# Real and imaginary products summed in DRAM by accumulating transfers, in a fused attention and spectral filter kernel

## The chip, the cores and the metric

The kernel runs on one core of one Trainium2 chip. The metric is the device time of one execution in microseconds (us). Times of single instructions come from one profiled execution.

## The reference, cut to what matters

The kernel computes a neighbourhood attention block with an MLP over x of shape (4, 56, 56, 128), a gated attention over the same rows, and a spectral filter bank. The change touches only the last part:

```
Vf = rfft(phi, n=8192);  Uf_p = rfft(u, n=8192);  Uf_m = rfft(u * sgn, n=8192)
U_plus  = irfft(Vf * Uf_p)[:, :sl]
U_minus = irfft(Vf * Uf_m)[:, :sl] * sgn
out = einsum('btkd,k,kde->bte', U_plus, sigma ** 0.25, M_phi_plus)
    + einsum('btkd,k,kde->bte', U_minus, sigma ** 0.25, M_phi_minus)
    + (three shifted products with M_u)
```

One of four filter sets is chosen by a softmax over weights and noise. The kernel works in the frequency domain: for each frequency s it forms a complex 128x128 matrix G(s) from phi, sigma and the M matrices, multiplies the spectrum U(s) of the rows by it, and transforms the products Y(s) back. Y is complex. Its real part is rU rG - iU iG and its imaginary part rU iG + iU rG, so four real products go into two sums.

## The kernel before, in words

The order of the work is written out by hand, one list per stage, and every engine walks the same list. Four stages follow each other: the front (attention, MLP), the spectrum of the rows, the filter stage (class Filters, L1313 to L1526), from about 870 to 1634 us, and the inverse (class Inverse, L1560 to L1871), to the end.

**Filter stage.** 784 frequencies (slots) lie in 14 groups P of 56. A group has four steps s (56 steps in all): two halves of the output columns e, and two of the filter sets each. In a step PE makes 32 filter tiles G (L1379, L1382), ACT and DVE copy them from PSUM by turns (L1420, L1434), and PE multiplies U by them in 28 sums (L1401). The four products of a slot are not combined: the rows of a sum are U's real and imaginary part apart (p, r, b), its columns are G's real and imaginary part (k, e). After each odd step ACT copies the four PSUM banks of sums to the tile YS (L1426), and SP stores YS by four transfers of 224 KB to the DRAM tensor Yd (L1498), 28 stores in all. POOL prepares U with its twiddle factors (planes, L1451 to L1479) for 28 half groups. The tile for U has three buffers.

**Inverse.** Eight groups n (batch b, pair pp) of the rows have two steps t = 2n, 2n+1 each. For n the slots of Yd are loaded into YL[n % 2] by eight transfers of 392 KB (load_y, L1529). For n = 0 and 1 they are issued in the filter stage, the last rows of them after the last store has landed. For later n SP issues them when the buffer is free. DVE combines YL into YC (L1707): one addition or subtraction of 98x1024 for each of two halves and two parts k, and a copy of row 0 for its special slots (L1711). POOL forms sums and differences BF of the odd slots (butterfly, L1733), for n = 0 DVE does the second half. In step t PE does:

- turn(t-1) (L1628), a reversal of rows of the tile DF, after the odd part of t;
- the even part (L1608): banks "two" and "four", from YC;
- the odd part (L1621): banks "straight" and "crossed", from BF.

ACT copies "two" (PB, L1692) and scales the odd banks (SP, L1678, L1680), POOL adds these to DVE's GH (outer, L1761, L1762) in EO (L1839). DVE's loop over t runs in this order: whole(t-1), which makes SC (L1770), DF (L1775) and NT (L1776); outer(t); turned(t-2) (L1795); kept(t-1) (L1786); then a combine. kept and turned add the result to the tile RN, which holds the rows of the attention part; kept(2n) waits until RN(n) has been loaded (load_out, L1545, 2 x 392 KB). ACT stores RN(n-1) in step t = 2n+1 (L1850).

In SP's list of the inverse, step n waits for the combines of n, issues the loads of n+2, waits for the store of RN(n-2) and issues load_out(n).

Of the kernel before, what the change touches and what calls it, by code (L numbers as in the profile page):

```python
# [11 lines left out]
G = 98  # L12
# [225 lines left out]
class Front:  # L238
# [222 lines left out]
    def load_columns(self, e):  # L461
# [8 lines left out]
        e.dma_start(col[:, 6:10], D["b_fc1"].rearrange("(i p) -> p i", p=128), allow_slow_non_contiguous=True).then_inc(S["d_rest"], 16)  # L470
        for i, a in enumerate((D["b_proj"], D["b_fc2"], D["bq"], D["bk"], D["bv"])):
            e.dma_start(self.rowb[:, 1 + i, :], row_of(a)).then_inc(S["d_rest"], 16)

    def scalar(self, e):
        S, col = self.S, self.col
        for k, n in self.order:
# [83 lines left out]
            elif k == "p_pick":  # L560
                e.wait_ge(S["pz"], 1)
                e.activation(self.tm[:, 4:8], self.tm[:, 0:4], ACT.Exp, accum_out=self.tm[:, 17:18]).then_inc(S["pexp"], 1)
# [11 lines left out]
            elif k == "p_root":  # L574
                for i in range(2):
                    if i == 0:
                        e.wait_ge(S["d_pick"], 16 * 7)
                    else:
                        e.wait_ge(S["root"], 1)
                    e.activation(self.sg[:, i + 1:i + 2], self.sg[:, i:i + 1], ACT.Sqrt).then_inc(S["sqrt"], 1)  # L580
            elif k in ("f_dft", "f_part"):
                self.spec.scalar(e, k, n)
            elif k == "p_vf":
                e.wait_ge(S["vmul"], 2 * n + 2)
                if n == 0:
                    e.wait_ge(S["root"], 2)
# [27 lines left out]
    def vector(self, v):  # L614
        S, ch = self.S, self.dve_steps
        for k, n in self.order:
# [121 lines left out]
            elif k == "p_root":  # L738
                sg = self.sg
                for i in range(2):  # L740
                    s, r = sg[:, i:i + 1], sg[:, i + 1:i + 2]
                    v.wait_ge(S["sqrt"], i + 1)
# [8 lines left out]
                    v.tensor_scalar(r, r, 0.5, None, ALU.mult).then_inc(S["root"], 1)  # L751
# [17 lines left out]
    def pick(self, v):  # L769
# [8 lines left out]
        v.tensor_scalar(z, z, tm[:, 16:17], None, ALU.subtract).then_inc(S["pz"], 1)  # L778
        v.wait_ge(S["pexp"], 1)
# [151 lines left out]
    n_rest = 16 * (2 + 1 + 5 + 3 + 3)  # L931

    def setup(self, e, part):
# [15 lines left out]
        e.dma_start(self.ident[:, :], D["c_id"]).then_inc(S["d_first"], 16)  # L949
# [134 lines left out]
    pz pexp mixed mturn cast rest sqrt root vmul vf vcut  # L1084
# [228 lines left out]
class Filters:  # L1313
# [44 lines left out]
    def tensor(self, e):  # L1358
        S = self.S
        for k, s, i in self.order():  # L1360
# [24 lines left out]
            elif k == "sums":  # L1385
# [10 lines left out]
                if par == 0 and i % 8 == 0 and s >= 2:  # L1396
                    e.wait_ge(S["ys"], 4 * (s // 2 - 1) + bk + 1)
# [17 lines left out]
    def scalar(self, e):  # L1415
        S = self.S
        for k, s, i in self.order():
# [33 lines left out]
    def planes(self, q, c, u, u7, w, n):  # L1451

        S, ch = self.S, self.pool_steps
        a = u7.rearrange("d s (m r b) -> d s m r b", m=7, r=2)[:, :, 0:3]
# [24 lines left out]
        q.tensor_tensor(im, im, spare, ALU.subtract).then_inc(S["u7"], 1)  # L1479

# [533 lines left out]
```

## Time and profile before

| | |
|---|---|
| median of 3 runs | 1827.38 us (1826.96 to 1833.2) |
| profiled execution, its own time | 1826.17 us |
| its span | 1824.9 us |
| mean granted TensorE clock | 0.964 |
| PE, DVE, ACT, POOL busy | 1696.0, 1352.8, 1228.7, 727.5 us |

Engines: PE is TensorE's matmul, PEld its weight load, DVE is VectorE, ACT ScalarE, POOL GpSimd, SP SyncE. SPq and ACTq are DMA issues of these engines. A row's line number (L1401) is that of the kernel before. "idle before <-" names what ended the idle time before an instruction. "issue" there is time in which the engine waited for nothing that the profile shows. PEclk is the granted TensorE clock, where 1.00 is 2.4 GHz and 0.50 is 1.2 GHz. DMA share is the mean busy share of the 16 DMA engines.

### The profile page before, as it was taken

How to read it: one execution, taken by the hardware profiler on the slowest of the kernel's cores; microseconds unless marked ns; L12 is line 12 of the kernel's file. 1: busy time of each engine (PE TensorE's matmuls, PEld its weight loads, DVE VectorE, ACT ScalarE, POOL GpSimd, SP SyncE). 2: the span in 40 equal slices, each digit the busy share in tenths (PEclk: the TensorE clock that was granted, in tenths of full speed). 3: DMA queues.
4: the chain of work that ended last, by engine and by line, in shares of the span. 5: the costliest groups of instructions: out<-in, count | busy, mean ns of one | idle time of the engine just before them, and what ended most of it. 6: DMA issues, size and time to landing. Idle time of an engine off the chain costs nothing.

```text
span 1824.9 us, 76133 instructions
## 1 busy us (share of the span) xinstructions
PE 1696.0 (93%) x32219; PEld 1355.5 (74%) x32219; DVE 1352.8 (74%) x3789; ACT 1228.7 (67%) x2667; POOL 727.5 (40%) x877
## 2 busy tenths in 40 slices
PE   5999999999999998989899999999999999986887
PEld 3566676666766766888788888888888888874555
DVE  2677778888867765795677777777777777747998
ACT  5788888887877754646677777777777777751221
POOL 6545556555645543130532213333222333104553
PEclk8899999999999997998999999999999999997888
DMA  4422333433233323386322122222212222268763
GB/s 118 116 80 76 106 85 93 110 85 99 75 86 92 85 72 91 110 275 209 118 68 56 37 69 69 63 53 59 64 40 69 68 57 59 58 162 218 221 194 105
DMA packets 266056, 181.12 MB, mean 99 GB/s; under 512 B 39944, under 2 KB 263078, under 8 KB 264218
## 3 DMA queue, kind: packets, MB, share of 16 engines
q1 hardware_dynamic: 257154, 169.07, 33.8%
q10 hardware_dynamic: 7924, 6.02, 1.1%
q8 instruction: 256, 4.19, 1.0%
q0 software_dynamic: 640, 1.16, 0.2%
q14 instruction: 82, 0.67, 0.1%
HBM read 105.65 MB, written 70.63 MB: 97 GB/s over the span
## 4 chain that ended last, share of the span: by engine, by line
PE 63%; DVE 16%; issue 9%; POOL 5%; ACT 4%; DMA 2%; SPq 1%; DVEq 0%; POOLq 0%; ACTq 0%
PE banks L1401 19%; PE banks L1379 10%; PE banks L1382 9%; PE banks L409 6%; DVE zone L610 4%; PE banks L403 3%; PE banks L368 2%; PE banks L358 2%; PE banks L416 2%; PE banks L382 1%; DVE YC L1707 1%; PE banks L1608 1%; PE banks L456 1%; DVE st L597 1%; DVE W L652 1%
## 5 line engine op out<-in xcount | busy, mean ns | idle before, releaser
L1434 DVE COPY Gm<-banks 128x448 f32<-128x448 f32 x896 | 552.8, 639 | 206.9 <-PE banks L1379 126.7
L1420 ACT ACTIVATE Gm<-banks 128x448 f32<-128x448 f32 x896 | 515.2, 628 | 195.3 <-PE banks L1379 149.1
L1401 PE MATMUL banks<-Gm,U 128*32 128x128 f32 x12544 | 514.4, 274 | 9.7 <-POOL U L1479 5.1
L1401 PEld LDWEIGHTS banks<-Gm,U 128*32 128x32 f32 x12544 | 336.6, 110 | 53.0 <-issue 48.1
L1382 PE MATMUL banks<-V,zone 118*32 118x224 bf16 x7040 | 292.3, 259 | 0.0
L872 POOL TENSOR_TENSOR W<-W,mx 128x280 f32<-128x280 f32 x196 | 130.3, 665 | 227.6 <-DVE mx L659 227.4
L1379 PE MATMUL banks<-V,zone 118*128 118x224 bf16 x1824 | 215.4, 261 | 3.2 <-issue 2.7
L1379 PEld LDWEIGHTS banks<-V,zone 118*128 118x128 bf16 x1824 | 157.1, 98 | 49.7 <-issue 41.8
L1382 PEld LDWEIGHTS banks<-V,zone 118*32 118x32 bf16 x7040 | 192.8, 96 | 1.3 <-issue 1.1
L522 ACT ACTIVATE W<-W,mx 128x140 f32<-128x140 f32 x392 | 156.2, 402 | 0.3
L610 DVE TENSOR_SCALAR zone<-XR,zone 112x128 f32<-112x128 f32 x336 | 152.1, 497 | 5.1 <-POOL zone L834 3.2
L368 PE MATMUL banks<-ident,W 128*98 128x128 f32 x784 | 124.3, 282 | 21.9 <-ACT W L532 12.6
L652 DVE CUSTOM_DVE_ANT_0 W<-banks,zone 128x140 f32<-128x140 f32 x392 | 102.6, 298 | 54.7 <-PE banks L358 28.1
L532 ACT ACTIVATE W<-banks 98x512 f32<-98x512 f32 x196 | 114.7, 585 | 30.2 <-PE banks L368 29.8
L1460 POOL COPY U<-UL 128x896 f32<-128x896 f32 (+2 forms) x14 | 24.2, 1726 | 274.1 <-PE banks L1401 203.9
L368 PEld LDWEIGHTS banks<-ident,W 128*98 128x98 f32 x784 | 87.8, 131 | 60.7 <-POOL W L872 35.4
L1463 POOL TENSOR_TENSOR U<-UL 128x448 f32<-128x448 f32 x14 | 25.2, 1798 | 250.1 <-PE banks L1401 237.4
L834 POOL TENSOR_TENSOR zone<-zone 112x4 f32<-112x4 f32 x112 | 119.6, 1068 | 9.3
L597 DVE BATCH_NORM_STATS2 st<-XR 112x6 f32<-112x128 f32 x448 | 107.4, 281 | 8.4 <-DMA XR<-in_x_dram 5.8
L409 PE MATMUL banks<-zone 128*112 128x128 f32 x896 | 105.7, 277 | 2.9 <-ACT zone L554 2.8
L409 PEld LDWEIGHTS banks<-zone 128*112 128x112 f32 x896 | 101.2, 179 | 8.3 <-ACT zone L554 7.4
L358 PE MATMUL banks<-kP,qT 32*32 32x140 f32 x3136 | 94.5, 296 | 10.9 <-DVE mx L652 10.8
(183 smaller groups left out, 2785.4 us busy)
## 6 DMA issues: line engine op xcount, KB each, us to landing
Yd<-YS SPq DMA_DIRECT2D x112, 224.0 KB, 4.4
W<-Vd SPq DMA_DIRECT2D x392, 49.0 KB
UL<-Ud SPq DMA_DIRECT2D x27, 448.0 KB, 4.0
zone<-Yd SPq DMA_DIRECT2D x30, 392.0 KB
YL<-Yd SPq DMA_DIRECT2D x30, 392.0 KB
zone<-Mbf SPq DMA_DIRECT2D x28, 256.0 KB
Vd<-W SPq DMA_DIRECT2D x56, 112.0 KB
T<-XR SPq DMA_DIRECT2D x28, 224.0 KB, 2.6
```

The costliest lines, as they stand in the source:

```text
L358: ins = e.matmul(self.psum[2 + j][c:c + 32, 0:140], self.qT[b % 2][hs, at + 32 * j:at + 32 * j + 32], self.kP[b % 2][hs, r:r + 10, 8 * x:8 ...
L368: ins = e.transpose(self.psum[4][0:G, 256 * c + 128 * j:256 * c + 128 * j + 128], self.PN[n % 3][:, j, G * c:G * c + G], self.ident[:, :])
L409: ins = e.matmul(p[0:TB, 128 * m:128 * m + 128], self.HT[:, f, TB * m:TB * m + TB], self.wf2[:, f, :], start=f == 0, stop=f == 3)
L522: ins = e.activation(self.PB[n % 3][:, j, :], self.SB[n % 3][:, j, :], ACT.Exp, bias=self.mx[n % 4][:, j:j + 1], scale=-1.0, accum_out=sel ...
L597: ins = v.bn_stats(self.st[:, m, :], self.row(g)[:, 128 * m:128 * m + 128])
L610: ins = v.tensor_scalar(x[:, m, 0:128], self.row(g)[:, 128 * m:128 * m + 128], self.mv[k][g % 2][:, m, 0:1], self.rs[k][g % 2][:, m:m + 1] ...
L872: q.tensor_tensor(self.inner(self.PN[n % 3]), self.PB[n % 3], r, ALU.mult).then_inc(S["pn"], 1)
L1379: ins = e.matmul(pt[:, q, :], M, V, start=True, stop=True)
L1382: ins = e.matmul(pt[32 * x:32 * x + 32, q, :], M[:, 32 * x:32 * x + 32], V, start=True, stop=True, tile_position=(0, 32 * x))
L1401: ins = e.matmul(p[32 * x:32 * x + 32, :], self.U7[(2 * P + ch) % 3][:, sl, 8 * (3 - q):8 * (3 - q) + 32], self.Gm[:, par, r:r + 2, :], st ...
L1420: e.activation(dst, src, ACT.Copy).then_inc(S["gm_act"], 1)
L1434: v.tensor_copy(dst, src).then_inc(S["gm_dve"], 1)
```

## The change

- The rows of a sum are now (p, b, r): real rows on even partitions, imaginary rows on odd ones. For that POOL's planes write U in another order, with two copies (or two pairs of additions) per half group where there was one.
- The eviction of the sums is split: two banks on ACT, two on DVE, each by two instructions of half the columns. The second multiplies the columns of G's imaginary part by a sign per partition (-1 on odd ones), which is loaded at the start.
- SP stores the even partitions to Yd by one transfer, and the odd ones, with the two column halves exchanged, to a second tensor Zd by two. For group 0 a fourth small transfer puts the special rows of slot 0 into Yd directly.
- A transfer issued by POOL adds Zd to Yd in DRAM with accumulation, one per group of 56 frequencies; the last group has two, one after each store. It waits for the store to have landed and for the accumulation before it.
- Yd holds sums now, half as many bytes. load_y loads 196 KB instead of 392, YL has three buffers of half the size, and the loads wait for the accumulations. PE, ACT and POOL read YL directly; YC and the DVE combines are gone.
- In SP's list of the inverse, step n waits for "crossed" of t = 2n+1, issues the loads of n+3 into the freed buffer, and then goes on to load_out(n) as before.
- Some semaphores are merged (p_pick and its neighbours), with the same order of events.

```diff
     def scalar(self, e):
...
-            elif k == "sums" and s % 2 and i in (7, 15, 23, 27):
...
-                e.activation(self.YS[:, 4 * bk:4 * bk + n, :].rearrange("p g x -> p (g x)"),
-                             self.banks[:, 2048 + 512 * bk:2048 + 512 * bk + 128 * n], ACT.Copy).then_inc(S["ys"], 1)
+            elif k == "sums" and s % 2 and i in (7, 23):
+                dst, src = self.evict_sums(e, s, i)
+                e.activation(dst[:, :, 0:64], src[:, :, 0:64], ACT.Copy)
+                e.activation(dst[:, :, 64:128], src[:, :, 64:128], ACT.Copy, scale=self.D["wsel"][:, 16:17]).then_inc(S["ys_act"], 1)
...
     def vector(self, v):
...
+            elif k == "sums" and s % 2 and i in (15, 27):
+                dst, src = self.evict_sums(v, s, i)
+                v.tensor_copy(dst[:, :, 0:64], src[:, :, 0:64])
+                v.tensor_scalar(dst[:, :, 64:128], src[:, :, 64:128], self.D["wsel"][:, 16:17], None, ALU.mult
+                                ).then_inc(S["ys_dve"], 1)
...
     def planes(self, q, c, u, u7, w, n):
...
+        for r in range(2):
+            to, of = x7[:, :, :, r], s4[:, :, :, r]
+            if c < NCH // 2:
+                q.tensor_copy(to, of)
+            else:
+                src = x7
+                q.tensor_tensor(to[:, 0:n:2], of[:, 0:n:2], of[:, 1:n:2], ALU.add)
+                ch.tick(q.tensor_tensor(to[:, 1:n:2], of[:, 0:n:2], of[:, 1:n:2], ALU.subtract))
...
+    def add_up(self, q, c):
+
+        S, D, P = self.S, self.D, c // 2
+        q.wait_ge(S["d_y"], stored(c + 1))
+        if P:
+            q.wait_ge(S["d_ya"], added(c) + 16 * (c == NCH - 1))
+        rows = slice(896 * P + (0 if P else 16), 896 * P + 896)
+        hs = slice(0, 2) if P < NCH // 2 - 1 else slice(c % 2, c % 2 + 1)
+        q.dma_start(D["Yd"][rows, hs], D["Zd"][rows, hs], accum_op=ALU.add, max_dma_last_dim=4096).then_inc(S["d_ya"], 16)
...
     def sync(self, e):
...
-                for x in range(4):
-                    e.dma_start(D["Yd"][56 * P:56 * P + 56].rearrange("(g s) r h x -> s r g h x", s=4)[x, :, :, half, :],
-                                self.YS[32 * x:32 * x + 32, :, :]).then_inc(S["d_y"], 16)
+                to, up = (D[y][896 * P:896 * P + 896, half].rearrange("(g i) x -> i g x", i=64) for y in ("Yd", "Zd"))
+                e.dma_start(to, self.YS[0:128:2]).then_inc(S["d_y"], 16)
+                for k in range(2):
+                    e.dma_start(up[:, :, 64 - 64 * k:128 - 64 * k], self.YS[1:128:2, :, 64 * k:64 * k + 64]
+                                ).then_inc(S["d_y"], 16)
...
         e.wait_ge(S["d_ylh"], 64)
-        e.wait_ge(S["d_y"], 64 * NCH)
+        e.wait_ge(S["d_ya"], added(NCH))
...
         e.wait_ge(S["sums"], 28 * Filters.STAGES)
+        for a in range(8):
+            load_y(e, D, D["YL2"], a, 1, 0).then_inc(S["d_yl2"], 16)
         load_out(e, D, S, 0)
...
     def first_blocks(self, v):
         S = self.S
         v.wait_ge(S["d_yl0"], 64)
-        self.combine(v, 0, 1, 0, 0, 2)
-        self.combine(v, 0, 1, 1, 0, 2).then_inc(S["yc"], 1)
         v.wait_ge(S["d_ylh"], 96)
...
     def vector(self, v):
-        self.combine_early(v, 0)
         self.first_blocks(v)
         self.outer(v, 0)
-        self.combine_late(v, 1)
         self.outer(v, 1)
-        self.combine_early(v, 1)
...
-            if t < 14:
-                n = t // 2 + 1
-                if t % 2:
-                    self.combine_late(v, n + 1) if n + 1 < 8 else None
-                else:
-                    self.combine_early(v, n)
...
     def sync(self, e):
         S, D = self.S, self.D
         for n in range(8):
-            if n + 2 < 8:
-                e.wait_ge(S["yc"], 2 * n + 3)
-                for a in (4, 5, 6, 7, 0, 1, 2, 3):
-                    load_y(e, D, self.YL[n % 2], a, (n + 2) // 2, n % 2).then_inc(S[f"d_yl{n % 2}"], 16)
+            if n + 3 < 8:
+                e.wait_ge(S["idft"], INVERSE_DONE["crossed", 2 * n + 1])
+                for a in range(8):
+                    load_y(e, D, self.YL[n % 3], a, (n + 3) // 2, (n + 3) % 2).then_inc(S[f"d_yl{n % 3}"], 16)
             if n:
                 if n >= 2:
                     e.wait_ge(S[f"d_o{n % 2}"], 32 * ((n - 2) // 2 + 1))
```

## Rows read from the trace of the kernel before

**Rows 1.** Busy us by stretch: PE, PEld, DVE, ACT, POOL; clock, DMA share, GB/s.
```profile
880.00:1608.00 728.00, 721.15 (x20726) 635.24 (x20728) 534.38 (x865) 536.71 (x971) 224.51 (x214) 1.00 0.24 59
1660.00:1815.00 155.00, 126.78 (x477) 86.22 (x478) 150.24 (x185) 35.50 (x57) 82.46 (x58) 0.87 0.64 183
```

**Rows 2.** Waits of PE and PEld, 880 to 1635: us, times, longest.
```profile
PE banks L1401 <- POOL U L1479: 5.1, 3, 2.6
PE banks L1401 <- issue: 4.3, 4, 2.9
...
PEld banks L1379 <- ACT Gm L1420: 5.2, 26, 0.2
```

**Rows 3.** DVE's groups, 1685.2 to 1773.3: busy us, mean ns, idle before.
```profile
L1786 DVE SCALAR_TENSOR_TENSOR RN<-NT,wsel,RN 98x256 f32<-98x256 f32 x16 | 18.6, 1204 | 0.0
L1707 DVE TENSOR_TENSOR YC<-zone 98x1024 f32<-98x1024 f32 x8 | 11.7, 1478 | 0.0
...
L1711 DVE COPY YC<-zone 1x256 f32<-1x256 f32 x5 | 4.3, 855 | 0.2
```

**Rows 4.** Timeline of PE in the inverse: start us, us.
```profile
1653.31 6.05 PE L1621 MATMUL banks<-zone 98*98 98x256 f32 x16 [8.45 <-DVE zone L1739]
1668.30 2.00 PE L1628 MATMUL banks<-DF,rev 98*98 98x512 f32 x2 [8.94 <-DVE DF L1775]
...
1679.52 1.02 PE L1628 MATMUL banks<-DF,rev 98*98 98x512 f32 x2
...
1683.83 3.62 PE L1621 MATMUL banks<-zone 98*98 98x256 f32 x16
...
1768.20 3.62 PE L1621 MATMUL banks<-zone 98*98 98x256 f32 x16
...
1811.51 3.62 PE L1621 MATMUL banks<-zone 98*98 98x256 f32 x16
1814.96 1.02 PE L1628 MATMUL banks<-DF,rev 98*98 98x512 f32 x2
```

**Rows 5.** Timeline of the queues of SP and ACT, one burst.
```profile
1707.37 6.99 SPq L1533 DMA_DIRECT2D YL<-Yd  x8
1722.91 0.81 SPq L1545 DMA_DIRECT2D RN<-T  x2
...
1712.06 1.15 ACTq L1850 DMA_DIRECT2D out_dram<-RN  x2
```

**Rows 6.** Busy time by stretch, four stretches of the inverse.
```profile
1708.30:1722.70 14.40, 13.16 (x42) 8.70 (x43) 14.33 (x20) 3.00 (x5) 6.37 (x5) 0.76 0.93 275
1718.00:1722.00 4.00, 4.00 (x18) 2.73 (x17) 4.00 (x6) 1.87 (x4) 1.57 (x2) 1.00 0.95 337
1710.00:1716.00 6.00, 6.00 (x13) 3.47 (x12) 6.00 (x8) 0.60 (x1) 2.67 (x2) 0.50 0.94 240
1668.50:1676.00 7.50, 7.50 (x18) 4.58 (x19) 7.43 (x8) 0.60 (x1) 3.27 (x3) 0.55 0.99 248
```

**Rows 7.** Timeline of DVE near the end.
```profile
1802.30 1.40 DVE L1770 SCALAR_TENSOR_TENSOR SC<-banks,zone,EO 98x512 f32<-98x512 f32 x2
1803.73 0.69 DVE L1775 TENSOR_TENSOR DF<-SC 98x512 f32<-98x512 f32 x1
...
1813.75 0.87 DVE L1786 SCALAR_TENSOR_TENSOR RN<-NT,wsel,RN 98x256 f32<-98x256 f32 x2
```

**Rows 8.** Timeline of POOL, start of the inverse.
```profile
1663.91 5.37 POOL L1839 TENSOR_TENSOR EO<-GH,SP 98x512 f32<-98x512 f32 x4
```

**Rows 9.** Timeline of PE and SP at the hand-over.
```profile
1621.26 0.67 PE L1379 MATMUL banks<-V,zone 118*128 118x224 bf16 x5 [2.55 <-issue]
...
1636.69 5.82 SPq L1498 DMA_DIRECT2D Yd<-YS  x4
1647.55 0.75 SPq L1533 DMA_DIRECT2D zone<-Yd  x2
```

**Rows 10.** DMA issues of POOL in the front: KB each, us to landing.
```profile
Vd<-kP POOLq DMA_DIRECT2D x6, 93.0 KB, 3.3
```

More of the change, by code:

```diff
@@ L1396, in tensor @@
                 if par == 0 and i % 8 == 0 and s >= 2:
-                    e.wait_ge(S["ys"], 4 * (s // 2 - 1) + bk + 1)
+                    e.wait_ge(S["ys_dve" if bk % 2 else "ys_act"], 2 * (s // 2 - 1) + bk // 2 + 1)
                 for x in range(4):
@@ L1438, in gpsimd @@
         for k, c, _ in self.order():
+            if k == "store" and (c % 2 or c == NCH - 2):
+                self.add_up(q, c)
             if k != "load":
@@ L1522, in sync, with stored, added @@
         e.wait_ge(S["sums"], 28 * Filters.STAGES)
+        for a in range(8):
+            load_y(e, D, D["YL2"], a, 1, 0).then_inc(S["d_yl2"], 16)
         load_out(e, D, S, 0)
-FILTER_SIGNALS = "gmm gm_act gm_dve u7 sums ys d_m0 d_m1 d_m2 d_m3 d_v0 d_v1 d_tw0 d_tw1 d_ul d_y d_ylh d_yl0 d_yl1 d_iv d_rev".split()
+FILTER_SIGNALS = "gmm gm_act gm_dve u7 sums ys_act ys_dve d_m0 d_m1 d_m2 d_m3 d_v0 d_v1 d_tw0 d_tw1 d_ul d_y d_ya d_ylh d_yl0 d_yl1 d_yl2 d_iv d_rev".split()
 def load_y(e, D, yl, a, b, pp, p0=0, p1=G):
     first, step = (G * a, 1) if a < 4 else (392 + 196 * (a // 2 - 2) + a % 2, 2)
-    rows = D["Yd"][first + step * p0:first + step * (p1 - 1) + 1:step]
-    src = rows.rearrange("s (p r b) h x -> s b p r (h x)", r=2, b=4)[:, b, 2 * pp:2 * pp + 2]
-    return e.dma_start(yl[a // 4][p0:p1, 1024 * (a % 4):1024 * (a % 4) + 1024].rearrange("s (p r x) -> s p r x", p=2, r=2), src)
+    rows = D["Yd"].rearrange("(s p b) h x -> s b p (h x)", p=4, b=NB)[first + step * p0:first + step * (p1 - 1) + 1:step]
+    src = rows[:, b, 2 * pp:2 * pp + 2]
+    return e.dma_start(yl[a // 4][p0:p1, 512 * (a % 4):512 * (a % 4) + 512].rearrange("s (p x) -> s p x", p=2), src)
+def stored(c):
+    return 64 * min(c, 2) + 48 * max(c - 2, 0)
+def added(c):
+    return 16 * (c // 2 + (c == NCH))
 def out_rows(A, n, k):
@@ L1600, in wait_bank, with part @@
             e.wait_ge(self.S[name], n)
+    def part(self, n, a):
+        return self.YL[n % 3][a // 4][:, 512 * (a % 4):512 * (a % 4) + 512].rearrange("p (x k e) -> p k x e", k=2, e=64)
     def even(self, e, kind, t):
@@ L1642, in tensor @@
             self.odd(e, "crossed", t, (0,))
-        e.wait_ge(S["yc"], 3)
+        e.wait_ge(S["first"], 2)
         for t in range(2):
@@ L1743, in first_blocks @@
         v.wait_ge(S["d_yl0"], 64)
-        self.combine(v, 0, 1, 0, 0, 2)
-        self.combine(v, 0, 1, 1, 0, 2).then_inc(S["yc"], 1)
         v.wait_ge(S["d_ylh"], 96)
-        self.steps.tick(self.combine(v, 0, 1, 0, 2, 4))
-        self.steps.tick(self.combine(v, 0, 1, 1, 2, 4))
-        v.wait_ge(self.steps.sem, self.steps.n)
         v.wait_ge(S["gmm"], 32 * (Filters.STAGES - 2))
-        self.steps.tick(self.butterfly(v, 0, 1, 0))
-        self.butterfly(v, 0, 1, 1).then_inc(S["yc"], 1)
+        self.butterfly(v, 0, 1, 0).then_inc(S["first"], 1)
+        self.butterfly(v, 0, 1, 1).then_inc(S["first"], 1)
     def outer(self, v, t):
@@ L1868, in sync @@
         e.wait_ge(S["d_o1"], 32 * 3 + 96)
-INVERSE_SIGNALS = "yc idft half gh spun eo bf fixed rows tdif tmm turned kept d_rn0 d_rn1 d_o0 d_o1".split()
+INVERSE_SIGNALS = "first idft half gh spun eo bf fixed rows tdif tmm turned kept d_rn0 d_rn1 d_o0 d_o1".split()
 def program(nc, x, ln1_w, ln1_b, w_qkv, b_qkv, rpb, w_proj, b_proj, ln2_w, ln2_b, w_fc1, b_fc1, w_fc2, b_fc2,
```

139 lines of the change are left out of this document (60 added, 79 removed).

## The prediction

> **What bounds the kernel now.** I read the busy time by stretch first. From 880 to 1608 us the kernel is in its filter stage: PE is busy for 721 of 728 us at full clock, DVE for 534 and POOL for 225 [rows 1]. What DVE, ACT, POOL or the queues do there costs only what makes PE wait. From 1660 to 1815 us it is in the inverse, and the roles are turned: DVE is busy 150 of 155 us, PE 127 at a mean clock of 0.87 [rows 1]. So the change (fewer DVE instructions in the inverse, more transfers and split evictions in the filter stage) takes work from the engine that is full in the one stage and must not disturb PE in the other.
>
> The next view is DVE's groups over four whole frequency groups n of the inverse, 1685.2 to 1773.3 us. The reader should see L1707: two equal groups (the one into the other YL buffer is not shown) of 8 combines of 98x1024 each, together 23.4 us, and the row copies L1711, of which the first five take 4.3 us and nine take about 7.3 [rows 3]. That is 30.7 us of the 88.1, or 7.7 per n. All of it goes. The PE timeline then gives the rhythm. With T(n) for the end of the "crossed" product of step t = 2n+1, L1621 starts at 1683.83 for n=1, 1768.20 for n=5 and 1811.51 for n=7 [rows 4]: T(1) to T(5) is 84.4 us (21.1 per n), T(5) to T(7) 43.3. Where PE is not kept waiting, turn and even part of one t take 4.31 us (1679.52 to 1683.83) and the odd part 3.45 (1811.51 to 1814.96) [rows 4]: 7.76, or 15.5 per n. DVE without the combines needs 21.1 - 7.7 = 13.4 to 14 per n. So PE would become the bound, at 15.5 to 15.9, if nothing else were late.
>
> **What is late instead.** This is the step on which I decide. In the new `sync` of the inverse, SP waits at step n for T(n), then issues eight loads for n+3, and only then `load_out(n)`, the two loads of RN(n). For n = 1 to 4 that wait stands ahead of them; n = 5 to 7 have no YL load. DVE's `kept(2n)` needs RN(n), and it stands in the DVE program right after `outer(2n+1)` and `turned(2n-1)`, work that is done at T(n). Before, the queue was released by the combines, one DVE iteration earlier: its eight loads go out at 1707.37, RN's at 1722.91, and `kept` had no wait in this stretch (idle before L1786 is 0.0) [rows 3, 5]. Behind the waiting `kept(2n)` on DVE stand `whole(2n+1)` and its difference DF; PE's `turn(2n+1)` waits for DF, and PE has only even and odd of t = 2n+2 to do before it.
>
> How long is RN(n) behind T(n)? At T(n) SP issues 8 x 196 KB (1.61 MB, half of today's 8 x 392), ACT issues the store of RN(n-1), 0.80 MB, within 2 us (today that store is at 1712.06, inside the load burst [rows 5]), and SP then 0.80 MB for RN(n), last in its queue. Today's burst of 4.01 MB ran from 1708.30 to 1722.70 at 275 GB/s and share 0.93, 0.9 us after its first issue [rows 5, 6]. 3.21 MB at 275 GB/s is 11.7 us; with 0.1 for SP's release, 0.9 to the first bytes and 0.2 at the end RN(n) is there L = 12.9 us after T(n). Bounds: 10.7 if all runs at the 337 GB/s of its second part [rows 6]; 8.4 if besides the store cost nothing (2.41 MB); 14.6 at 240 GB/s, which is 13.4 us of transfer.
> The Trainium skill (DMA: Bandwidth & Descriptors, Issuing engines are not separate DMA queues) says that transfers started by SP, ACT and GpSimd run on the same 16 DMA engines and interleave. The burst agrees, its share is already 0.93 with ACT's store in it. By the rule L is 12.9; were the store on engines of its own, L would be 10.0 and the total 11.6 us less.
>
> From RN(n) on: `kept` 0.87 (L1786, no POOL beside it), two SC and DF 2.1, and gaps, to the turn: 3.2 [rows 7]. Then turn, even and odd. After PE's idle gap of 8.94 us before 1668.30 the clock was 0.55 in 1668.5 to 1676, and from turn to the next turn (1679.52) it took 11.2 instead of 7.76 [rows 4, 6]. PE's gap in the new cycle is about 8 us (P less 15.5 and this 3.4), so I take 11.2. P = 12.9 + 3.2 + 11.2 = 27.3 us per n for n = 1 to 4. Ends: 10.7 + 3.2 + 9.6 = 23.5 (a mild clock loss as behind the shorter gaps) and 29.0.
>
> **The sum for the inverse.** T(1) to T(5): 4 x 27.3 - 84.4 = +24.8. T(5) to T(7): 31.5 - 43.3 = -11.8 (two cycles of 15.5 and 0.5 for DVE instructions stretched beside POOL). Start: PE's first turn is at 1668.30, 15.0 after the first complete odd products at 1653.31 [rows 4]. POOL's four butterflies for n=1 wait for a DVE combine today, and the EO operations behind them begin at 1663.91, each 1.34 [rows 8]. New: the butterflies begin 0.5 before those products, four at 1.4 (the same 98x512 operation) take 5.6, and 4.4 from EO to turn, as now: 9.5, so -5.5. After T(7) nothing changes. Together +7.5.
>
> **Hand-over from the filter stage.** Today the last YS store is issued from 1636.69, because SP sat behind the 8 YL loads, and its landing releases SP at 1647.55 [rows 9]; 5.8 us later (3.1 load, 1.3 combine, 1.3 butterfly) PE goes on at 1653.31. New: half as many bytes are ahead, and the 2.55 us in which PE got no instructions at 1618.7 [rows 9], after 6 us of saturated loads, I take as gone. Sums then end 2.5 earlier, the three store parts go out at 1632.4 and land at 1640.5. Now the accumulating transfer is put in, on the path: POOL's wait, issue, 448 KB read twice and written once. No row shows one. Bounds: 3.3, the landing of a plain 93 KB transfer issued by POOL [rows 10], and 13, twice what three passes of 0.46 MB need at the 240 GB/s of a burst's first part [rows 6], and 1 for issuing. I take 7, those three passes once and 1 for issuing. Load 3.1 and butterfly 1.3: 1652.0, -1.3. POOL's first butterflies now stand behind its wait for the store; they are ready about 1645, before the last rows, and cost nothing more.
> The Trainium skill (DMA: Bandwidth & Descriptors, Anatomy of one DMA) fits a GpSimd transfer with 2.0 us and bytes over 436 GB/s: estimate from the page 3.1 us for 459 KB, 3.9 less than mine, near the low row. It is a fit for plain transfers; no run here shows an accumulating one yet.
>
> **The filter stage.** Evictions: the four YS evictions on ACT become two split ones on ACT and two on DVE, each two instructions. Today the one in the middle of the stage already makes the next LDWEIGHTS wait for ACT, 26 times 0.2 us [rows 2], without breaking PE's rhythm of 3.32 us. DVE has less room there; I take +1.5 in all, from 0 to 8 (0.3 in each of 28 odd stages). POOL's planes get one or two instructions more each. Only those of the first three chunks are on the path, where PE waits 5.1 us for POOL today [rows 2]: +1.0, from 0.5 to 3. Later ones have 4 us of slack in a stage of 13.3. The 14 accumulations before the last have 53 us each; on POOL their wait stands behind all planes that are due. I cost them nothing; what it costs if they starve PE of instructions is a rival. Fewer bytes are stored for good, nothing is waited for. One small load on ACT and the new sign column: nothing.
>
> **Sum**: +7.5 - 1.3 + 2.5 = +8.7. The profiled execution took 1826.17 us (span 1824.9), 1.2 under the median of 1827.38; on the median it is 1836.1, I say 1836. About 0.5% (9 us) is what a measurement of this kernel tells from no change, so this lies at the upper edge of "the same".
>
> **Rivals.** (a) The RN wait is short: L 8.4, clock loss as now: P 22.8, 18 us less than my sum: 1818. For it: 337 GB/s in half of today's burst. Against: the first half at 240. (b) The RN wait does not bite at all, PE runs at 15.5 per n: 4 x 11.8 = 47 less: about 1789. For it: DVE's 7.7 per n is real. Against: the order in `sync` and `vector`. (c) Slower: the accumulations saturate the DMA engines behind each store burst, and PE runs out of instructions as at 1618.7, 2.5 us in 13 pairs: +33, 1869; it decides from the point where store and accumulation together stay saturated for over 6 us. Against: today's 28 store bursts, leave 4.3 us of such idle time before L1401 in the whole stage, 2.9 of it at once [rows 2]. A slow last accumulation (13) adds 6 to any case. (d) The page's 3.1 us for the accumulation is inside my own range.
>
> **Chances.** Mine 0.57, own range 1822 to 1850, split by the 1836.5 line: 0.02 faster, 0.24 same, 0.31 slower. (a) 0.17: 0.11 faster, 0.06 same. (b) 0.11, faster. (c) 0.13, slower. The rest 0.02, same. Together faster 0.24, same 0.32, slower 0.44. Range 1804 to 1858: it leaves out (b) and the upper half of (c), somewhat under 0.2.
>
> **What would show it.** Right: DVE idle for 8 to 12 us before the `kept` operation, released by a DMA RN<-T, four times; PE's turns late by as much with a clock of 0.5 behind them; the last cycles at 15.5; no L1707. Wrong: no DMA wait on RN (b), or "issue" idle of PE over 10 us in all before 1608 (c), or a last accumulation over 10 us.

## The result and the profile after

The changed kernel took 1859.18 us (median of 4, 1855.6 to 1862.15) against 1827.18 for the kernel before, and is slower by 32 us. The ratio over all executions is 1.0165, with a 95% interval of 1.0135 to 1.0195 (that of the two medians is 1.0175). Forecast were 1836 us and 1804 to 1858; the median lies 1.2 us above that range, which is less than single executions differ. The profiled execution took 1859.99 us (span 1858.7); what follows is read from it against the 1824.9 us span before.

Busy time by stretch comes first, as in [rows 1] (us, then PE, PEld, DVE, ACT and POOL busy, clock, DMA share, GB/s):

```profile
880.00:1608.00 728.00, 703.53 (x19984) 615.80 (x19988) 540.93 (x939) 506.60 (x938) 239.48 (x268) 0.99 0.31 70
1660.00:1815.00 155.00, 101.42 (x374) 68.97 (x373) 71.48 (x105) 28.78 (x47) 63.89 (x49) 0.80 0.46 122
```

In the filter stage PE does 19984 matmuls in the 728 us, not 20726. In the inverse DVE, which was full before (150 of 155 us), is busy 71 us, and no other engine is full either (PE 101): something is waited for. The waits of PE from 880 to 1640 us answer to [rows 2]; the last row is DVE's largest wait from 1640 to 1860:

```profile
PE banks L1402 <- issue: 10.8, 12, 3.1
PE banks L1383 <- issue: 9.3, 8, 1.9
PE banks L1402 <- POOL U L1497: 5.1, 3, 2.7
PE banks L1380 <- issue: 0.5, 2, 0.4
...
DVE RN L1804 <- DMA RN<-T: 64.2, 5, 16.4
```

"issue", PE waiting for nothing that the profile shows, grew from 7.0 to 20.6 us in all. And `kept` on DVE now waits for the loads of RN: four waits of 15.5 to 16.4 us and one of 0.4. The timeline of PE in the inverse answers to [rows 4] (L1657 is the even part, L1670 the odd one, L1682 the turn):

```profile
1655.83 7.15 PE L1657 MATMUL banks<-zone 98*98 98x256 f32 x32
1668.30 8.91 PE L1670 MATMUL banks<-zone 98*98 98x256 f32 x32 [5.32 <-ACT zone L1753]
1682.61 2.00 PE L1682 MATMUL banks<-DF,rev 98*98 98x512 f32 x2 [5.40 <-DVE DF L1793]
...
1697.88 3.62 PE L1670 MATMUL banks<-zone 98*98 98x256 f32 x16
...
1720.01 2.00 PE L1682 MATMUL banks<-DF,rev 98*98 98x512 f32 x2 [10.75 <-DVE DF L1793]
...
1814.19 3.62 PE L1670 MATMUL banks<-zone 98*98 98x256 f32 x16
...
1845.25 3.62 PE L1670 MATMUL banks<-zone 98*98 98x256 f32 x16
```

The rows give the whole difference in four pieces. The end of the last sums is taken as the start of the first even part, which follows them without a gap: L1657 at 1655.83, and in the kernel before L1608 at 1634.03.

| piece, us | before | after | difference | predicted |
|---|---|---|---|---|
| start to the end of the last sums | 1634.03 | 1655.83 | +21.8 | 0 (+2.5 evictions and planes, -2.5 stall) |
| from there to T(1) | 49.80 | 42.05 | -7.75 | -4.3 (hand-over +1.2, start -5.5) |
| T(1) to T(5) | 84.4 | 116.3 | +31.9 | +24.8 |
| T(5) to T(7) | 43.3 | 31.1 | -12.2 | -11.8 |
| sum | | | +33.8 | +8.7 |

**The wait for RN.** One cycle, T(1) to the next turn. First SP's queue [rows 5], then the chain of waits, then DVE:

```profile
1701.53 6.39 SPq L1569 DMA_DIRECT2D YL<-Yd  x8
1707.96 0.92 SPq L1591 DMA_DIRECT2D RN<-T  x2
```

```profile
1707.96 0.42 SPq L1591
1708.43 8.41 DMA RN<-T
```

```profile
1716.94 0.88 DVE L1804 SCALAR_TENSOR_TENSOR RN<-NT,wsel,RN 98x256 f32<-98x256 f32 x2 [15.70 <-DMA RN<-T]
1717.73 1.41 DVE L1788 SCALAR_TENSOR_TENSOR SC<-banks,zone,EO 98x512 f32<-98x512 f32 x2
1719.17 0.69 DVE L1793 TENSOR_TENSOR DF<-SC 98x512 f32<-98x512 f32 x1
```

T(1)'s product ends at 1701.50, SP goes 0.03 us later, and RN is there 15.4 us after T(1). The burst by windows [rows 6] and, in the last row, the clock behind the gap:

```profile
1702.00:1716.00 14.00, 7.26 (x33) 5.12 (x31) 0.00 (x0) 3.22 (x6) 3.71 (x3) 0.89 0.86 229
1716.00:1730.00 14.00, 9.99 (x30) 6.57 (x31) 12.99 (x20) 1.02 (x2) 5.30 (x4) 0.62 0.01 2
```

229 GB/s over 14 us is 3.21 MB: the eight YL loads, ACT's store and RN's loads, exactly the bytes that the prediction counted. PE still works 7.3 of these 14 us, mostly on the even and odd part of t = 4, and then stops. From 1716 to 1730, until the next T(n), the DMA engines stand idle (share 0.01). So the burst and the work that waits for it take turns.

**The accumulations.** The DMA issues (KB each, median us from issue to landing), and the queues with their packets, MB and share:

```profile
Yd<-Zd POOLq DMA_DIRECT2D x12, 896.0 KB, 9.4
...
Yd<-Zd POOLq DMA_DIRECT2D x2, 448.0 KB, 6.7
```

```profile
q0 software_dynamic: 5616, 13.99, 3.9%
...
q8 instruction: 256, 4.19, 0.9%
```

One of them, the twelfth: POOL issues it at 1563.91, together with a load of UL by SP, and PE stops at 1568.2:

```profile
1563.91 0.88 POOL L1507 DMA_DIRECT2D Yd<-Zd  x1
```

```profile
1567.41 0.82 PE L1402 MATMUL banks<-Gm,U 128*32 128x128 f32 x19
1571.36 0.42 PE L1402 MATMUL banks<-Gm,U 128*32 128x128 f32 x5 [3.13 <-issue]
```

```profile
1564.00:1568.00 4.00, 4.00 (x125) 3.58 (x115) 2.89 (x6) 3.08 (x7) 0.79 (x1) 1.00 0.65 140
1568.00:1571.00 3.00, 0.23 (x7) 0.00 (x0) 0.28 (x1) 0.05 (x1) 0.00 (x0) 1.00 1.09 226
1571.00:1575.00 4.00, 3.65 (x69) 3.21 (x72) 2.50 (x5) 1.69 (x4) 0.00 (x0) 0.74 0.22 43
1575.00:1579.00 4.00, 4.00 (x104) 3.60 (x100) 2.18 (x4) 2.20 (x5) 0.00 (x0) 0.83 0.01 4
```

The DMA engines are full until 1571; PE executes nothing from 1568.2 to 1571.4, and after its gap the granted clock is 0.74 and 0.83 for 8 us. Each of the 14 accumulations from 952 to 1642 us has such a stall behind it, of 0.5 to 3.1 us (mean 1.3), which ends 6.6 to 10.4 us after the issue.

What PE lacks can be read from the packets of q8, the queue of kind "instruction". The trace keeps their times. There are 256 of 16 KiB, and PE and PEld executed 64438 instructions together, 252 for each packet, so I take them for PE's instructions. From 940 to 1640 us a packet starts 4.15 us behind the one before it (median). At this stall one starts at 1561.26 and the next only at 1569.01, 7.75 us later; it ends at 1569.98, and PE goes on 1.4 us after that. It is the same in all 23 "issue" waits of PE from 880 us to the end of the sums: PE goes on 1.3 to 1.5 us after a packet of q8 has ended. Behind the 14 accumulations that packet starts 5.4 to 8.2 us after the one before it. In the kernel before it is 1.3 to 1.6 us, in six waits from 940 us on.

### The profile page after: what moved, and what is told of

It is laid out like the page before. It is cut to its first block, busy times and chain, and to the rows that moved or that the text cites. A ratio compares the mean times of both kernels' runs of the same rounds, so it can differ in the third digit from the quotient of the medians.

```text
span 1858.7 us, 76265 instructions
## 1 busy us (share of the span) xinstructions
PE 1696.0 (91%) x32219; PEld 1354.4 (73%) x32219; DVE 1321.0 (71%) x3851; ACT 1215.6 (65%) x2667; POOL 739.4 (40%) x937
## 3 DMA queue, kind: packets, MB, share of 16 engines
q0 software_dynamic: 5616, 13.99, 3.9%
## 4 chain that ended last, share of the span: by engine, by line
PE 67%; DVE 12%; issue 6%; POOL 5%; ACT 4%; DMA 4%; SPq 2%; DVEq 0%; POOLq 0%; ACTq 0%
PE banks L1402 20%; PE banks L1380 10%; PE banks L1383 9%; PE banks L409 5%; DVE zone L611 4%; PE banks L403 3%; PE banks L1657 2%; PE banks L368 2%; PE banks L358 2%; PE banks L1670 2%; DMA RN<-T 2%; PE banks L416 2%; PE banks L382 1%; SPq L1569 1%; DVE st L598 1%
## 5 line engine op out<-in xcount | busy, mean ns | idle before, releaser
L1442 DVE COPY Gm<-banks 128x448 f32<-128x448 f32 x896 | 549.5, 637 | 204.4 <-PE banks L1380 116.3
L1402 PE MATMUL banks<-Gm,U 128*32 128x128 f32 x12544 | 519.7, 275 | 17.1 <-issue 11.8
L1402 PEld LDWEIGHTS banks<-Gm,U 128*32 128x32 f32 x12544 | 341.6, 110 | 61.7 <-issue 56.2
L1383 PE MATMUL banks<-V,zone 118*32 118x224 bf16 x7040 | 297.0, 260 | 9.3 <-issue 9.3
L1383 PEld LDWEIGHTS banks<-V,zone 118*32 118x32 bf16 x7040 | 195.5, 97 | 12.2 <-issue 12.0
L1476 POOL COPY U<-UL 128x448 f32<-128x448 f32 (+2 forms) x28 | 26.1, 961 | 272.7 <-PE banks L1402 197.9
L1479 POOL TENSOR_TENSOR U<-UL 128x224 f32<-128x224 f32 x28 | 28.0, 1000 | 259.7 <-PE banks L1402 229.1
L358 PE MATMUL banks<-kP,qT 32*32 32x140 f32 x3136 | 94.2, 296 | 10.9 <-DVE mx L653 10.8
```

The source lines that it names most:

```text
L358: ins = e.matmul(self.psum[2 + j][c:c + 32, 0:140], self.qT[b % 2][hs, at + 32 * j:at + 32 * j + 32], self.kP[b % 2][hs, r:r + 10, 8 * x:8 ...
L1383: ins = e.matmul(pt[32 * x:32 * x + 32, q, :], M[:, 32 * x:32 * x + 32], V, start=True, stop=True, tile_position=(0, 32 * x))
L1402: ins = e.matmul(p[32 * x:32 * x + 32, :], self.U7[(2 * P + ch) % 3][:, sl, 8 * (3 - q):8 * (3 - q) + 32], self.Gm[:, par, r:r + 2, :], st ...
```

## Experiments

Each kernel ran in three rounds beside the kernel before. Where a kernel differs from the changed one, only the difference is shown. Times in us are medians; waits and ends of stages are of one profiled execution, which can lie up to 14 us from the median (the table at the end gives its time). Theories after the result: O, the order of SP's list makes T(1) to T(5) slow; S, the accumulations stall PE; against O stand slower loads as such, against S the split evictions, POOL's planes and the mere traffic.

**rn_early**: the loads of RN(n) ahead of everything that step n waits for.

```
 for n in range(8):
+    if n:
+        if n >= 2:
+            e.wait_ge(S[f"d_o{n % 2}"], 32 * ((n - 2) // 2 + 1))
+        load_out(e, D, S, n)
     if n + 3 < 8:
         e.wait_ge(S["idft"], INVERSE_DONE["crossed", 2 * n + 1])
         for a in range(8): ... load_y ...
-    if n: ... load_out(e, D, S, n)
```

> The changed kernel, only with load_out(n) issued ahead of the wait for T(n) and the YL loads in SP's list. Theory W (the inverse is held by kept(2n) waiting for RN(n), 15.4 us behind T(n)): T(1) to T(5) falls from 116.3 us to about 62 to 64, PE at full clock, 15.5 to 16 a group; total about 53 us below the changed kernel, 1806. Rival Q (the loads themselves are too slow for the new rhythm: YL or RN loads come late whatever their order): T(1) to T(5) stays above 80, total above 1822. The filter stage is as in the changed kernel by both.

Measured 1800.6 us, ratio 0.9846 (0.9832 to 0.9861). T(1), T(5) and T(7) in its timeline of PE, and its wait for RN:

```profile
1692.26 3.62 PE L1670 MATMUL banks<-zone 98*98 98x256 f32 x16
...
1754.38 3.62 PE L1670 MATMUL banks<-zone 98*98 98x256 f32 x16
...
1785.44 3.62 PE L1670 MATMUL banks<-zone 98*98 98x256 f32 x16
```

```profile
DVE RN L1804 <- DMA RN<-T: 0.4, 2, 0.3
```

T(1) to T(5) is 62.1, T(5) to T(7) 31.1: PE's own rhythm of 7.76 throughout, as computed in the first part of the prediction. The order was worth 54.2 us.

**rn_first**: the wait for T(n) stays ahead, only the eight YL loads go behind load_out(n).

```
     e.wait_ge(S["idft"], INVERSE_DONE["crossed", 2 * n + 1])
-    8 x load_y(n + 3)
 load_out(e, D, S, n)
+8 x load_y(n + 3)
```

> The changed kernel, with the wait for T(n) kept ahead of load_out(n), but load_out(n) ahead of the eight YL loads. It parts the two halves of the wait: if most of the 15.4 us is the queue in front of RN(n) (1.6 MB of YL), RN(n) lands 5 to 6 us behind T(n), in time for PE's next turn at about 7.8 behind it or 1 to 2 us late, and T(1) to T(5) is 64 to 74 us, total 1807 to 1817. If the wait for T(n) itself holds it, T(1) to T(5) stays above 95 us and the total above 1838.

Measured 1814.85 us, ratio 0.9929 (0.9908 to 0.9951). T(1) to T(5) is 76.8 us (1699.95 to 1776.72), and DVE waits 25.6 us for RN in five waits, 8.8 at most. So of the 54.2 us, 39.5 were the queue ahead of RN's loads and 14.7 the wait for T(n). The period is a little above the expected 64 to 74, and the profiled execution was the slowest of the six (1823.6). The medians divide the whole gain much the same: 44.3 and 14.3 of 58.6 us.

**before_rn_early**: the same move in the kernel before, where the loads of RN(n) now stand ahead of the wait for the combines.

```
+    if n: ... load_out(e, D, S, n)
     if n + 2 < 8: wait yc; 8 x load_y(n + 2)
-    if n: ... load_out(e, D, S, n)
```

> The kernel before with the loads of RN(n) moved ahead of the wait for the second turn and of the YL loads; no accumulations, nothing else. It tells whether the 1800.6 us of the same move in the changed kernel are owed to that kernel's smaller loads (eight of 196 KB a half) or to the order alone. Own theory: before, RN was loaded in time, and the half period of 21 to 22 us is set by VectorE and by the loads of 3.1 MB a pair, so the move gives nothing here or costs a little: 1824 to 1834, T(1) to T(5) 84 us +- 3. Rival: the order was a cost before as well, and T(1) to T(5) falls under 75 us: 1800 to 1817.

Measured 1828.74 us, ratio 0.9997 (0.9979 to 1.0015); T(1) to T(5) is 87.3 us (1680.87 to 1768.18) where it was 84.4, just above the expected 81 to 87. There the order costs nothing: `kept` had no wait for RN before [rows 3]. That the combines and their loads set the pace there is argued from DVE's 150 busy us of 155 [rows 1], not tried. What rn_early gains is therefore the change's own gain, set free.

**tiny_add**: every accumulation touches 16 of its 896 rows; the addition of the others is left out.

```
 hs = slice(0, 2) if P < NCH // 2 - 1 else slice(c % 2, c % 2 + 1)
+rows = slice(rows.start, rows.start + 16)
```

> The changed kernel with each accumulating transfer cut to 16 of its 896 rows: it leaves out the addition of all other rows, every wait and every other instruction stays. Theory S (the filter stage is 22 us longer since each accumulation keeps the DMA engines full for 6 to 9 us and PE gets its instructions late): idle time of PE by issue in the filter stage falls from about 21 us to under 7, the last sum ends about 20 us earlier, and with 4 to 5 us less at the hand-over the total is about 1834. Rival E (the split evictions, POOL's longer planes or the stores of 256 B pieces slow PE): the last sum ends at most 3 us earlier, total about 1852.

Measured 1833.89 us, ratio 1.0025 (1.0011 to 1.0039). The last sums end at 1630.67, 25.2 earlier than in the changed kernel and 3.4 earlier than before. Its waits of PE from 880 to 1640, and the landing:

```profile
PE banks L1402 <- issue: 1.8, 3, 0.7
PE banks L1383 <- issue: 1.8, 3, 0.8
PE banks L1380 <- issue: 0.6, 1, 0.6
```

```profile
Yd<-Zd POOLq DMA_DIRECT2D x13, 16.0 KB, 2.8
```

S holds, and evictions and planes cost nothing. Of the 25.2 us, 16.4 are issue waits (20.6 less 4.2). The rest lies in the matmuls. From 940 to 1608 one took 35.15 ns of PE (648.41 us by 18448), in tiny_add 34.74 (664.02 by 19116): 0.41 ns times the 21408 matmuls of the stage is 8.8 us. A lower clock explains less than half of it. From 940 us to the end of the sums, cut in stretches of 4 us, the changed kernel's granted clock is below 0.97 in three, behind its two longest stalls:

```profile
1460.00:1464.00 4.00, 4.00 (x69) 3.09 (x61) 1.93 (x4) 1.89 (x4) 0.00 (x0) 0.57 0.04 7
1572.00:1576.00 4.00, 4.00 (x83) 3.75 (x85) 2.73 (x6) 2.22 (x4) 0.00 (x0) 0.61 0.03 6
1576.00:1580.00 4.00, 4.00 (x117) 3.42 (x109) 2.78 (x5) 2.66 (x6) 0.00 (x0) 0.96 0.01 4
```

At full clock these stretches would have done the same work in 3.4 us less, an estimate from the three rows (4 us by 0.43, 0.39 and 0.04). The other 5.4 us are matmuls that took longer at a granted clock of 0.97 or more; why is not shown.

**plain_copy**: the transfer copies Zd over Yd instead of adding; the addition is left out, reads fall from two to one.

```
-q.dma_start(D["Yd"][rows, hs], D["Zd"][rows, hs], accum_op=ALU.add, max_dma_last_dim=4096)
+q.dma_start(D["Yd"][rows, hs], D["Zd"][rows, hs], max_dma_last_dim=4096)
```

> The changed kernel with the accumulating transfers made plain copies from Zd to Yd, same rows, same queue, same waits: it leaves out the addition. If it is the accumulation (a second read, the adding) that makes the burst long, the copies land in about 5 to 6 us instead of 9.4 and the filter stage is 12 to 20 us shorter, total 1838 to 1846. If any 0.9 MB DRAM to DRAM transfer on that queue does it, the filter stage stays within 4 us of the changed kernel's, total 1853 to 1860.

Measured 1844.87 us, ratio 1.0106 (1.0074 to 1.0138). Sums end at 1640.66, issue waits are 12.4 us:

```profile
Yd<-Zd POOLq DMA_DIRECT2D x12, 896.0 KB, 5.5
```

By the ends of the sums a plain transfer costs 10 of the 25 us, and that it accumulates, and takes 9.4 instead of 5.5 us, costs the other 15. By the medians it is 11 and 14.

**split_evict**: the kernel before with nothing but the split eviction of YS.

```
-four evictions on ACT (i = 7, 15, 23, 27), one instruction each
+ACT: i = 7, 23; DVE: i = 15, 27; two instructions each, columns 0:64 and 64:128
```

> The kernel before with one edit alone: two of the four evictions of sums per slab go to ScalarE, two to VectorE, each as a copy for the real and a copy for the imaginary half, as in the changed kernel; no accumulations, loads as before. The prediction costs this at +1.5 us (1829). Own theory: 1827 to 1831, last sums within 2 us of 1634.0, the inverse unchanged. Rival E (the evictions on VectorE, behind its Gm work, hold TensorE's banks at each slab and make up a good part of the 21.8 us by which the sums end later): 1835 to 1845. Since the changed kernel with its accumulations cut to 16 rows ended its sums at 1630.7, rival E has little left; a gain of up to 3 us is what that number would give.

Measured 1823.67 us, ratio 0.9986 (0.9972 to 1.0001). My +1.5 us was wrong in sign if anything: in the profiled execution the last sums end at 1628.86, 5.2 us earlier than before and outside the expected 2 us.

```profile
1626.91 1.95 PE L1401 MATMUL banks<-Gm,U 128*32 128x128 f32 x62 [1.06 <-issue]
```

**half_add**: one accumulation of 448 KB after each store, 28 instead of 15.

```
-if k == "store" and (c % 2 or c == NCH - 2):
+if k == "store":
-hs = slice(0, 2) if P < NCH // 2 - 1 else slice(c % 2, c % 2 + 1)
+hs = slice(c % 2, c % 2 + 1)
```

> Each accumulation of 896 KB after the second store of a pair is cut in two of 448 KB, one after each store, so that no burst is longer than about 6.5 us (the last two of the changed kernel, 448 KB each, landed in 6.7 us, the 896 KB ones in 9.4); the bytes are the same. Theory S (what costs the filter stage 25 us is the length of a stretch in which the DMA engines are full, at whose end TensorE has no instructions): the last sums end 10 to 20 us earlier than the changed kernel's 1655.8, TensorE's issue waits fall from 20.6 us to under 10, time 1840 to 1850. Theory B (it is the number of bytes that the accumulations move, however they are cut): no difference, 1859 +- 3. The period of the inverse is not touched by either: T(1) to T(5) stays 116 us.

Both theories missed: 1864.85 us, ratio 1.0217 (1.0189 to 1.0245), 5.7 above the changed kernel. The sums end at 1669.32, 13.5 later still, but in the slowest of the four executions (1869.75).

```profile
PE banks L1402 <- issue: 21.3, 15, 2.7
PE banks L1383 <- issue: 11.7, 11, 2.3
...
PE banks L1380 <- issue: 0.7, 2, 0.4
```

```profile
q0 software_dynamic: 26144, 13.99, 6.0%
...
Yd<-Zd POOLq DMA_DIRECT2D x26, 448.0 KB, 7.8
```

Half the bytes take 7.8 of 9.4 us, so there are nearly twice as many long bursts. The edit changed a second thing, though: a row of one half is no longer contiguous with the next half, and the packets went from 5616 to 26144.

**small_desc** tells this apart: whole accumulations in as many packets.

```
-max_dma_last_dim=4096
+max_dma_last_dim=512
```

> The accumulations keep their 896 KB and their places, but the longest run of elements in one descriptor is cut from 4096 to 512. If TensorE's instruction fetch waits behind the long elements of the accumulation in each DMA engine (theory Q), shorter ones let it in sooner: issue waits under 12 us, time 1845 to 1855. If the fetch waits because the engines are full (theory S), more descriptors for the same bytes make the burst no shorter: landing at 9.4 us or more, time 1857 to 1870. If 512 elements is already what a row gives (a row of one half is contiguous over 512 floats or fewer), the packets stay 5616 and nothing changes, 1859 +- 3.

Measured 1857.01 us, ratio 1.0177 (1.0154 to 1.02); sums end at 1653.42, issue waits 21.1 us, 25936 packets, landing 10.9 us. Theory Q is refuted, and neither the packets nor the 1.5 us of longer burst matter. With packets and bytes alike, what is left for the 7.8 us by which half_add is slower (1864.85 less 1857.01) is that it has 28 long bursts and not 15.

**half_add_rn_early**: both edits.

> Both edits together: accumulations of 448 KB after every store, and the loads of RN(n) ahead of the wait for T(n) and of the eight YL loads. If the two costs add (the filter stage under theory S, the inverse by the order of SP's list), the sums end at 1636 to 1646 and T(1) to T(5) takes 62 us as with the RN loads moved alone: 1782 to 1792, better than the 1800.6 of that edit alone. If theory B holds, 1800 +- 3. If the two hide one another (the inverse then starts against a late last accumulation), 1792 to 1798.

Measured 1813.17 us, ratio 0.9929 (0.9903 to 0.9955), 10 executions from 1808 to 1827; its three theories had 1782 to 1803. T(1) to T(5) is 62.1, so that gain is there in full. The expected gain in the filter stage is not: the time is 12.6 us above rn_early's. (The sums end at 1676.38, but in the slowest execution, 1827.08.)

**spread_add**: seven accumulations of 128 rows, each behind the landing of the one before; the last two groups' halves stay whole.

```
-q.dma_start(D["Yd"][rows, hs], D["Zd"][rows, hs], accum_op=ALU.add, max_dma_last_dim=4096)
+for k in range(7):
+    part = slice(896 * P + (128 * k if P or k else 16), 896 * P + 128 * k + 128)
+    if k:
+        q.wait_ge(S["d_ya"], added(c) + 16 * k)
+    q.dma_start(D["Yd"][part, hs], D["Zd"][part, hs], accum_op=ALU.add, max_dma_last_dim=4096)
```

> The same bytes in the same thirteen places, each accumulation of 896 rows cut by rows into seven of 128, each waiting for the one before it; the last two (448 KB each) stay whole. They fall into the 34 us in which GpSimd is idle after each. So far 448 KB at a time (7.8 us each) made the last sums later still (1669.3 against 1655.8), shorter descriptors changed nothing, 16 rows at a time (2.8 us) cost nothing. Theory L (a burst costs TensorE one stall of about 1.5 us if it fills the DMA engines for longer than TensorE's instructions last, 5 us or so, and nothing if it is shorter): pieces of 128 rows are short and have gaps of 2 us between them, issue waits under 8 us, last sums at 1628 to 1638, time 1832 to 1843. Theory N (each accumulation costs, whatever its length, as twice as many cost more): 93 instead of 15, issue waits over 40 us, time over 1870. Rival B (bytes): last sums at 1650 to 1660, 1855 to 1863.

Measured 1845.99 us, ratio 1.0084 (1.0056 to 1.0113), 13 us better than the changed kernel with the same bytes. Its transfers, POOL's timeline of three pieces, and the stretch of 20 us in which they run:

```profile
Yd<-Zd POOLq DMA_DIRECT2D x90, 128.0 KB, 3.3
```

```profile
1060.93 0.79 POOL L1514 DMA_DIRECT2D Yd<-Zd  x1
1064.63 0.79 POOL L1514 DMA_DIRECT2D Yd<-Zd  x1 [2.90 <-DMA Yd<-Zd]
1068.11 0.76 POOL L1514 DMA_DIRECT2D Yd<-Zd  x1 [2.69 <-DMA Yd<-Zd]
```

```profile
1064.00:1084.00 20.00, 19.49 (x564) 17.05 (x560) 15.32 (x28) 14.42 (x28) 3.84 (x5) 1.00 0.53 104
```

The mean share over 20 us is no lower than in the changed kernel (0.49 from 1062.68 to 1082.68, behind its third accumulation). What differs is how it lies in time: there it is 0.98 for 5.3 us on end (1066.00 to 1071.30), here 0.55, 0.26, 0.28, 0.90 and 0.64 in stretches of 4 us. Issue waits fall to 10.1 us (880 to 1640); 2.9 more come after 1637.85, beside the first of the two accumulations that stayed whole. N (each accumulation costs) and B (bytes) are refuted. L is right in kind, too hopeful in size: sums end at 1643.84, not 1628 to 1638, in this profile, and at 1635.18 in the one of the next kernel, which has the same filter stage. Ends of the same stage scatter by some us (1652.9, 1655.8 and 1658.3 in three kernels with the changed one's). The edit changes two things at once, the length of a transfer and the gap behind it; no run has short ones without gaps.

**spread_rn_early**: both edits. It beats both kernels.

> The accumulations cut in seven and spread, and the loads of RN(n) ahead of the wait for T(n) and of the eight YL loads. If theory L holds and the two gains add: last sums at 1628 to 1638, T(1) to T(5) 62 us, T(5) to T(7) 31 us: 1773 to 1785. Theory N: over 1815. Rival B: 1798 to 1803.

Measured 1786.54 us, ratio 0.9766 (0.9737 to 0.9795); 1.5 above the expected range.

```profile
PE banks L1402 <- issue: 4.4, 5, 1.5
PE banks L1383 <- issue: 2.3, 6, 0.8
PE banks L1380 <- issue: 1.0, 3, 0.4
```

With 7.7 us of issue waits and 62.1 us from T(1) to T(5) (1675.50 to 1737.62), the summing in DRAM is worth 42 us over before_rn_early, the kernel before in the same order.

| kernel | accumulating transfers | landing | issue waits, 880 to 1640 | sums end | T(1) to T(5) | profiled us | median us |
|---|---|---|---|---|---|---|---|
| changed | 13 x 896 KB, 2 x 448 | 9.4 | 20.6 | 1655.8 | 116.3 | 1860.0 | 1859.2 |
| tiny_add | 16 rows each | 2.8 | 4.2 | 1630.7 | 117.3 | 1833.5 | 1833.9 |
| plain_copy | 13 + 2, not accumulating | 5.5 | 12.4 | 1640.7 | 115.8 | 1841.9 | 1844.9 |
| half_add | 28 x 448 KB | 7.8 | 33.7 | 1669.3 | 114.8 | 1869.8 | 1864.9 |
| small_desc | 13 + 2, more packets | 10.9 | 21.1 | 1653.4 | 115.4 | 1854.2 | 1857.0 |
| spread_add | 91 x 128 KB, 2 x 448 | 3.3 | 10.1 | 1643.8 | 118.2 | 1848.0 | 1846.0 |
| rn_early | as changed | 9.7 | 19.8 | 1652.9 | 62.1 | 1800.1 | 1800.6 |
| spread_rn_early | as spread_add | 3.4 | 7.7 | 1635.2 | 62.1 | 1783.3 | 1786.5 |

## Why the prediction was right or wrong

The time came out 23 us above the forecast and 1.2 us outside the range. The direction of each step of the inverse was right; one cost was put at nothing and was the second largest.

- **The deciding step, "What is late instead": right.** DVE waits for RN as described, after T(n), four times, for 15.5 to 16.4 us (the forecast said 8 to 12), and moving the loads takes the wait away. The term itself was mis-sized: L was 15.4, not 12.9, since the 3.21 MB moved at 229 GB/s and not at the 275 of a burst before; P came out at 29.1 (27.3 predicted, with its end at 29.0), +31.9 instead of +24.8. The 3.2 us from RN to the turn were 3.1, the 11.2 from the turn to the next T exact (1720.01 to 1731.21). Of the rates of before, the 240 GB/s of the first part of a burst was the nearer row.
- **DMA queues.** All 3.21 MB, ACT's store among them, passed before RN was there, at a share of 0.86. This is what the Trainium skill says (DMA: Bandwidth & Descriptors, Issuing engines are not separate DMA queues), and the L of 10.0 that would follow from separate ones is refuted.
- **T(5) to T(7)**: -12.2, predicted -11.8. Where no RN is late behind YL loads, PE goes at 15.5 per n.
- **Hand-over and start**: -7.75, predicted -4.3. The last accumulation, issued at 1663.36, released SP at 1669.95, 6.6 us against my 7; bounds and choice were good. The stores before it landed 7.5 us behind the sums, where I had 9.0; with the 0.4 us by which the accumulation was shorter that gives 1.9 of the 3.4 us. The other 1.5 us lie between SP's release and T(1): 8.3 us less than before, where I had 6.8 less. The Trainium skill's fit (same page, Anatomy of one DMA) gives 3.1 us for it as an estimate; the plain copy of the same size landed in 4.3, the accumulation in 6.7 (median of two), so the fit is short for both.
- **The step that failed, in "The filter stage": "The 14 accumulations before the last have 53 us each [...] I cost them nothing."** It reasoned about POOL and about who waits for the result, and both were right. The price was paid by PE: the last sums end 25.2 us later than with accumulations of 16 rows. It is the mechanism of rival (c), at 1.2 us of stall (16.4 by 14) and 0.6 of longer matmuls (8.8 by 14) each instead of 2.5 of stall. The sign given for it, "issue" over 10 us before 1608, came true with 19.5. The price of (c) was not the mistake: its 1869 is my 1836 and 33, and 1836 with the measured 25 is 1861. The mistake was to give it 0.13 and to keep none of its cost in my own case, although nothing in one excludes the other: the filter stage and the inverse are different stages, and their costs add. The evidence against (c), 28 store bursts with 4.3 us of stalls, was of bursts whose stores landed in 4.4 us; with 9.4 us of accumulation behind them it did not bear.
- **Evictions and planes**: +2.5 predicted; nothing to a small gain measured (tiny_add ends its sums 3.4 earlier than before, of which 2.8 are fewer issue waits; split_evict has 0.9986).
- **Rivals (a) and (b)** need a short or no wait for RN; refuted. (b) gave 1789 for a kernel without that wait: it is what rn_early has (1800.6) with the stalls, and spread_rn_early (1786.5) with most of them gone.

What is shown of the mechanism, and what is not: cutting the transfers down takes the stalls away (tiny_add), and each stall ends right behind a packet of q8, which is late behind all 14 accumulations (5.4 to 8.2 us instead of 4.15). No experiment changed the fetching of instructions itself, and whether a late packet stood behind others in the DMA engines or was asked for late is open. Nor was it tried whether a burst has a sharp length above which it stalls PE. By how much the medians lie above tiny_add's, a transfer that lands in 3.3 us cost 0.13 us (12.1 by 91), in 5.5 us 0.8 (11.0 by 14), in 7.8 us 1.1 (31.0 by 28), in 9.4 us 1.8 (25.3 by 14) and in 10.9 us 1.7 (23.1 by 14). These are estimates; they put the whole difference down to the transfers in the background.

## What to carry to other kernels

A background transfer is free only if the DMA engines keep room: look at its landing time, not at how long its result is unneeded, and cut it into short pieces with a gap where PE must be fed. When loads are made smaller or later, read the issuing queue's list again: a small load that was early behind one wait can become the critical one behind another. And a cost in another stage is no rival to your main case: it can come on top of it, so it belongs in the sum or the range, not only in a small chance beside it.

## What the runs showed of the hardware

- An accumulating DRAM to DRAM transfer issued by GpSimd landed in 9.4 us for 896 KB, 6.7 for 448 (7.8 in half_add) and 3.3 for 128 KB; a plain one in 5.5 and 4.3 us for 896 and 448 KB. 4.6 times as many packets made 896 KB take 10.9 us. Issuing mostly took 0.88 us of GpSimd for 896 KB and 0.76 for 128 KB, 0.59 for the plain copy, and 1.22 in half_add and 1.69 in small_desc, which have more packets.
- Behind each of 14 accumulations PE stopped for 0.5 to 3.1 us; after the longest gap the granted clock was 0.74 and 0.83 for 8 us, and 1.00 again then.
- In each of the 23 "issue" waits of the changed kernel's filter stage PE went on 1.3 to 1.5 us after a packet of q8 (kind "instruction", 16 KiB) had ended. In 700 us of the filter stage (940 to 1640), 20 such packets start over 6 us behind the one before, against 9 in tiny_add and 8 in the kernel before.
- The changed kernel's burst of 3.21 MB ran at 229 GB/s, where the 4.01 MB of before ran at 275.
